# Late tiles of a mixture-of-experts kernel add the two parts of their up product on VectorE; one expert look-up; another front and end

## The reference

```python
ys = y * scale
d = rsqrt(einsum('bi,io->bo', ys * ys, weight * weight) + EPS)
xm = einsum('bsi,io->bso', x * ys[:, None, :], weight) * d[:, None, :]
...
router_logits = xm @ router_w.T + router_b + 0.1 * expert_weights    # from softmax(xm @ lang_w.T + lang_b)
top_p, top_i = top_k(softmax(router_logits), 2)                      # normalised to sum 1
h = gelu(einsum('bsd,edh->bseh', xm, w1) + b1)
expert_out = einsum('bseh,ehd->bsed', h, w2) + b2
return x + (top_p[..., None] * take_along_axis(expert_out, top_i[..., None], 2)).sum(2)
```

## Time and profile before

| | us |
|---|---|
| runs | 300.03, 297.01, 299.65 (median 299.65) |
| profiled execution | 296.99 |
| its span, first to last instruction | 295.2 |
| PE busy | 269.6 (91%) |
| PE weight loads busy | 221.2 (75%) |
| ACT, DVE, POOL busy | 195.2, 191.9, 175.4 |

### The profile page before, as it was taken

How to read it: one execution, slowest core, us unless ns; L and a number is a source line. 1 busy time by engine, 2 the same in 40 slices (tenths; PEclk the granted TensorE clock), 3 DMA queues, 4 the chain that set the end, 5 groups by cost and what they waited for, 6 DMA issues and landing times.

```text
span 295.2 us, 8972 instructions
## 1 busy us (share of the span) xinstructions
PE 269.6 (91%) x3065; PEld 221.2 (75%) x3065; DVE 191.9 (65%) x430; ACT 195.2 (66%) x425; POOL 175.4 (59%) x160
## 2 busy tenths in 40 slices
PE   7899967899999999999999999999999989999800
PEld 5778957788799998877778777777777767877500
DVE  2957787799999897656655655555656555556510
ACT  3355469499897997677667676766776756776500
POOL 8200026833366989887777877767787657464340
PEclk9799996999999999999999999999999999999985
DMA  6799995499862234645535555534535434332220
GB/s 160 290 400 388 368 323 155 129 404 450 294 191 41 38 59 69 95 76 88 93 56 91 75 93 73 79 68 76 90 59 80 88 56 74 53 39 25 32 35 1
DMA packets 39881, 39.53 MB, mean 134 GB/s; under 512 B 19920, under 2 KB 35744, under 8 KB 39680
## 3 DMA queue, kind: packets, MB, share of 16 engines
q1 hardware_dynamic: 32320, 28.56, 31.7%
q0 software_dynamic: 7488, 10.39, 21.9%
q10 hardware_dynamic: 32, 0.01, 0.0%
HBM read 27.61 MB, written 9.64 MB: 126 GB/s over the span
## 4 chain that ended last, share of the span: by engine, by line
PE 73%; DVE 9%; issue 6%; DMA 5%; POOL 4%; ACT 0%; DVEq 0%; POOLq 0%
PE ps L639 30%; PE ps L656 28%; DVE wsp L940 5%; PE ps L537 5%; DMA out<-onehot,idx 4%; PE ps L555 3%; POOL out L468 2%; PE ps L648 1%; POOL onehot L459 1%; PE ps L479 1%; PE ps L615 1%; DMA rows<-y_rows,idx 1%; PE ps L510 1%; PE ps L519 1%; DVE dv L871 1%
## 5 line engine op out<-in xcount | busy, mean ns | idle before, releaser
L639 PEld LDWEIGHTS ps<-onehot,wsp 128*128 (+1 forms) x1872 | 130.0, 98 | 37.4 <-issue 2.9
L639 PE MATMUL ps<-onehot,wsp 128*128 128x128 f16 x1872 | 154.4, 219 | 1.8 <-issue 1.5
L818 ACT ACTIVATE pay<-ps,cur 128x128 f32<-128x128 f32 x312 | 117.5, 463 | 54.9 <-issue 39.9
L656 PE MATMUL ps<-wsp,pay 128*128 (+1 forms) x616 | 139.4, 316 | 1.2 <-DVE pay L1102 1.2
L468 POOL DMA_INDIRECT out<-onehot,idx x39 | 68.7, 1762 | 28.9 <-POOL onehot L459 12.1
L1102 DVE SCALAR_TENSOR_TENSOR pay<-pay,cur 128x512 f16<-128x512 f32 x72 | 54.9, 762 | 28.8 <-ACT pay L806 26.6
L437 POOL DMA_INDIRECT rows<-y_rows,idx x39 | 49.4, 1266 | 22.4 <-issue 11.0
L459 POOL TENSOR_SCALAR onehot<-onehot,cur 128x256 f32<-128x256 f32 x37 | 43.0, 1161 | 25.6 <-DVE onehot L1120 21.6
L656 PEld LDWEIGHTS ps<-wsp,pay 128*128 128x128 f16 x616 | 45.3, 97 | 5.0 <-issue 1.6
L1096 DVE TENSOR_SCALAR pay<-pay,cur 128x512 f16<-128x512 f32 x36 | 19.4, 538 | 26.4 <-ACT pay L818 24.1
L806 ACT ACTIVATE pay<-pay,cur 128x512 f16<-128x512 f32 x36 | 26.0, 722 | 1.2
(11 more groups left out here) (177 smaller groups left out, 193.0 us busy)
## 6 DMA issues: line engine op xcount, KB each, us to landing
stage<-in_L_ffn_w SPq DMA_DIRECT2D x9, 1024.0 KB, 9.9
wsp<-in_L_ffn_w SPq DMA_DIRECT2D x7, 1024.0 KB, 11.8
y_rows<-pay SPq DMA_DIRECT2D x4, 512.0 KB, 9.4
wsp<-in_x SPq DMA_DIRECT2D x3, 512.0 KB, 8.1
b2bc<-in_L_ffn_b SPq DMA_DIRECT2D x1, 1024.0 KB, 9.4
rows<-y_rows,idx POOLq DMA_INDIRECT x39
out<-onehot,idx POOLq DMA_INDIRECT x39
wsp<-in_x SPq DMA_DIRECT2D x2, 256.0 KB, 5.8
```

The lines of the kernel that those rows point to most:

```text
L639: last = mm(ps[:, HB + (2 * j + g) % RING, c * P:(c + 1) * P], wsp[:, bass.ds(e, 1), o:o + P].rearrange("p a f -> p (a f)"), xsp[:, j % RI ...
L656: last = mm(ps[:, OB + j % 2, 0:width], hsp[:, (2 * j + g) % NH, part, c, :], wsp[:, bass.ds(e, 1), o + w:o + w + width].rearrange("p a f ...
L818: last = a.activation(to, ps[:, HB + (2 * j + g) % RING, c * P:(c + 1) * P], ACT.Gelu, bias=cur[:, j % CURS, cc:cc + 1], scale=cur[:, j % ...
```

## The change

- **Up, late tiles.** From tile LATE = 9 on, the second half (g = 1) takes x's high and low parts in one matmul of 256 columns, each part into PSUM columns of its own (banks 0 and 1): four matmuls instead of six. DVE adds the two (`sum_h`, a reduction of 128x1024 to 128x512 into `hsum`), and ACT's GELU reads `hsum` from SBUF. The first halves use banks 7 and 2, the rows banks 5, 6, 4 and 3 in turn (`LATE_H`, `LATE_O`). TensorE waits for `h_sum` before it writes the two banks again.
- **VectorE's order.** For late tiles `sum_h(j)`, `low_h(j, 0)`, then `rows_out(j - 2)` stand ahead of `high_h(j)`; before, `rows_out(j - 1)` and `low_h(j + 1, 0)` stood behind `low_h(j, 1)`.
- **Look-up.** BATCH is 31: all experts' numbers are read at once, on PE ahead of the loop.
- **Transposes.** TURNED is 7: tiles 7, 8 and 9 are turned by DMA.
- **Front.** Filler matmuls behind `sum_squares(0)` and `gram(2)`, ten instead of six behind `gram(3)`; the two DMAs of the probabilities go from the SP queue to POOL's; the weight half 7 is loaded ahead of them, `b2bc` ahead of the first gathers; the first up half stands ahead of the second transpose.
- **End.** For j = 36 and 37 the down half stands whole ahead of the up half; ACT weighs the last three tiles; the rows have five buffers (OUTS) instead of three.

```diff
+WIDE = range(E, NT)
...
+OUTS = 5
...
-WARM = 6
+WARM = 10
...
-TURNED = 10
+TURNED = 7
...
-EARLY = 8
-BATCH = 8
+BATCH = 31
+LATE = 9
+LATE_H = (7, 2)
+LATE_O = (5, 6, 4, 3)
...
+    hsum = stage[:, 0:2, 0:GH * P]
...
+    def bank_of_rows(j):
+        return OB + j % 2 if j < LATE else LATE_O[(j - LATE) % 4]
+
+    def bank_of_half(j, g):
+        return LATE_H[(j - LATE) % 2] if j >= LATE and g == 0 else HB + (2 * j + g) % RING
+
+
+    two_parts = ps[:, HB:HB + 2, :].rearrange("p b (c s n) -> p (b c) s n", s=2, n=P)
...
-        sp.wait_ge(p_ready, 1)
-        for b in range(NB):
-            sp.dma_start(y_tiles[:, b, :, D:ROW], payv[:, b * TB:(b + 1) * TB, D:ROW]).then_inc(p_written, 16)
         load_weights(7)
+        sp.wait_ge(p_written, 16 * NB)
+        sp.dma_start(b2bc[:, :, :].rearrange("p e d -> p (e d)"),
+                     b2.rearrange("(a e) d -> a (e d)", a=1).broadcast_to([P, E * D])).then_inc(b2_in, 16)
...
         load_weights(12)
-        sp.dma_start(b2bc[:, :, :].rearrange("p e d -> p (e d)"),
-                     b2.rearrange("(a e) d -> a (e d)", a=1).broadcast_to([P, E * D])).then_inc(b2_in, 16)
...
+        pool.wait_ge(p_ready, 1)
+        for b in range(NB):
+            g.dma_start(y_tiles[:, b, :, D:ROW], payv[:, b * TB:(b + 1) * TB, D:ROW]).then_inc(p_written, 16)
...
-            if j < NT - 2:
+            if j < NT - 3:
                 pool.wait_ge(o_read, j + 1)
-                g.tensor_scalar(outb[:, j % RING, :], outb[:, j % RING, :], cur[:, j % CURS, C_P:NCUR], None,
+                g.tensor_scalar(outb[:, j % OUTS, :], outb[:, j % OUTS, :], cur[:, j % CURS, C_P:NCUR], None,
                                 ALU.mult).then_inc(o_ready, 1)
                 pool.wait_ge(o_ready, j + 1)
             else:
-                pool.wait_ge(o_last, j - NT + 3)
+                pool.wait_ge(o_last, j - NT + 4)
...
         sum_squares(0)
+        pe.wait_ge(lg_read, T)
+        keep_warm(5, 1, 512)
...
         gram(2)
+        keep_warm(4, 1, 512)
         sum_squares(2)
...
         gram(3)
-        for _ in range(WARM):
-            mm(ps[:, RB, :], ones[:, :], onehot[:, 0:512], start=True, stop=True)
+        keep_warm(WARM, 1, 512)
...
+            if j >= LATE and g:
+                for w in range(2):
+                    for k in range(KD):
+                        o = w * HALF + k * F + (g * GH + c) * P
+                        last = mm(two_parts[:, c, 0:2 - w, :],
+                                  wsp[:, bass.ds(e, 1), o:o + P].rearrange("p a f -> p (a f)"),
+                                  xsp[:, j % RING, 0:2 - w, k, :], start=(w == 0 and k == 0), stop=(w == 1 and k == KD - 1))
+                return last
...
-            if j < EARLY:
+            if j not in WIDE:
                 steps = ((0, 0, D), (0, D, D), (1, 0, D))
...
                 elif g == 0:
                     wait_turned(pe, j)
+                elif j > LATE:
+                    pe.wait_ge(h_sum, j - LATE)
...
         transpose_rows(0)
+        blocks((0, 0), None)
         transpose_rows(1)
-        blocks((0, 0), None)
         blocks((0, 1), None)
         sum_squares(3)
         pe.wait_ge(te_ready, 1)
+        expert(E)
         for j in range(NT):
             if j + 2 < TURNED:
                 transpose_rows(j + 2)
-            blocks((j + 1, 0) if j + 1 < NT else None, (j - 1, 1) if j else None)
+            if NT - 4 < j < NT - 1:
+                blocks(None, (j - 1, 1))
+                blocks((j + 1, 0), None)
+            else:
+                blocks((j + 1, 0) if j + 1 < NT else None, (j - 1, 1) if j else None)
...
             if g == 0:
                 act.wait_ge(cur_ready, j + 1)
-            act.wait_ge(l1_done, 2 * j + g + 1)
+            if j >= LATE and g:
+                act.wait_ge(h_sum, j - LATE + 1)
...
+                up = (hsum[:, j % 2, :] if j >= LATE and g else ps[:, bank_of_half(j, g), :])[:, c * P:(c + 1) * P]
+                last = a.activation(to, up, ACT.Gelu,
                                     bias=cur[:, j % CURS, cc:cc + 1], scale=cur[:, j % CURS, C_GELU:C_GELU + 1])
...
+            if j == NT - 1:
+                weigh(NT - 3)
             gelus(j, 1)
...
+        def sum_h(j):
+            dve.wait_ge(l1_done, 2 * j + 2)
+            v.tensor_reduce(hsum[:, j % 2, :].rearrange("p (c n) -> p c n", c=GH), two_parts.rearrange("p c s n -> p c n s"),
+                            AX.X, ALU.add).then_inc(h_sum, 1)
...
-            if j >= RING:
-                dve.wait_ge(added, 16 * (j - RING + 1))
+            if j >= OUTS:
+                dve.wait_ge(added, 16 * (j - OUTS + 1))
...
         scale_weights(3)
         for j in range(NT):
-            if j == NT - 1:
+            if j >= LATE:
+                sum_h(j)
+                low_h(j, 0)
+            if LATE < j < NT - 2:
+                rows_out(j - 2)
+            if j >= NT - 3:
                 rows_out(j - 1)
             if j >= DIRECT:
                 high_h(j)
...
-            if 0 < j < NT - 1:
+            if 0 < j < LATE:
                 rows_out(j - 1)
-            if DIRECT <= j + 1 < NT:
+            if DIRECT <= j + 1 < LATE:
                 low_h(j + 1, 0)
```

More of the change, by code:

```diff
@@ L213, in adaln_moe @@
         xsp = onehot[:, 0:RING * 2 * D].rearrange("p (r s k n) -> p r s k n", r=RING, s=2, k=KD)
-        outb = onehot[:, RING * 2 * D:RING * 4 * D].bitcast(F32).rearrange("p (r n) -> p r n", r=RING)
+        outb = onehot[:, RING * 2 * D:(RING + OUTS) * 2 * D].bitcast(F32).rearrange("p (r n) -> p r n", r=OUTS)
         ps = ctx.enter_context(nc.psum_tensor("ps", [P, 8, 512], F32))
@@ L246, in adaln_moe @@
         gathered = [sem(f"gathered{r}") for r in range(ROWS)]
+        h_sum = sem("h_sum")
         t_done = sem("t_done"); turned = [sem(f"turned{r}") for r in range(RING)]; x_split = sem("x_split")
@@ L468, in _ @@
                 g.indirect_dma_start(out=out, out_offset=bass.IndirectOffsetOnAxis(ap=idx[:, j:j + 1], axis=0),
-                                     in_=outb[:, j % RING, :], in_offset=None,
+                                     in_=outb[:, j % OUTS, :], in_offset=None,
                                      compute_op=ALU.add).then_inc(added, 16)
@@ L638, in up_step @@
                     o = w * HALF + k * F + (g * GH + c) * P
-                    last = mm(ps[:, HB + (2 * j + g) % RING, c * P:(c + 1) * P],
+                    last = mm(ps[:, bank_of_half(j, g), c * P:(c + 1) * P],
                               wsp[:, bass.ds(e, 1), o:o + P].rearrange("p a f -> p (a f)"),
@@ L655, in down_step @@
                 for q, (part, w, width) in enumerate(steps):
-                    last = mm(ps[:, OB + j % 2, 0:width], hsp[:, (2 * j + g) % NH, part, c, :],
+                    last = mm(ps[:, bank_of_rows(j), 0:width], hsp[:, (2 * j + g) % NH, part, c, :],
                               wsp[:, bass.ds(e, 1), o + w:o + w + width].rearrange("p a f -> p (a f)"),
@@ L811, in gelus @@
                     act.wait_ge(cur_ready, j + 1)
-                act.wait_ge(l1_done, 2 * j + g + 1)
+                if j >= LATE and g:
+                    act.wait_ge(h_sum, j - LATE + 1)
+                else:
+                    act.wait_ge(l1_done, 2 * j + g + 1)
                 if j > DIRECT:
@@ L817, in gelus @@
                     to = hraw[:, (2 * j + g) % NH, c, :] if j < DIRECT else h32[:, g, c * P:(c + 1) * P]
-                    last = a.activation(to, ps[:, HB + (2 * j + g) % RING, c * P:(c + 1) * P], ACT.Gelu,
+                    up = (hsum[:, j % 2, :] if j >= LATE and g else ps[:, bank_of_half(j, g), :])[:, c * P:(c + 1) * P]
+                    last = a.activation(to, up, ACT.Gelu,
                                         bias=cur[:, j % CURS, cc:cc + 1], scale=cur[:, j % CURS, C_GELU:C_GELU + 1])
@@ L824, in weigh @@
             def weigh(j):
-                r = j % RING
+                r = j % OUTS
                 act.wait_ge(o_read, j + 1)
@@ L1105, in rows_out @@
             def rows_out(j):
-                r, e = j % RING, expert(j)
+                r, e = j % OUTS, expert(j)
                 if j == 0:
@@ L1114, in rows_out @@
                     return
-                v.scalar_tensor_tensor(out=outb[:, r, :], in0=ps[:, OB + j % 2, 0:D], scalar=cur[:, j % CURS, C_O:C_O + 1],
+                v.scalar_tensor_tensor(out=outb[:, r, :], in0=ps[:, bank_of_rows(j), 0:D], scalar=cur[:, j % CURS, C_O:C_O + 1],
                                        in1=b2bc[:, bass.ds(e, 1), :].rearrange("p a d -> p (a d)"),
-                                       op0=ALU.mult, op1=ALU.add).then_inc(o_read if j < EARLY else o_sum, 1)
-                if j >= EARLY:
-                    dve.wait_ge(o_sum, j - EARLY + 1)
-                    v.scalar_tensor_tensor(out=outb[:, r, :], in0=ps[:, OB + j % 2, D:2 * D], scalar=cur[:, j % CURS, C_O:C_O + 1],
+                                       op0=ALU.mult, op1=ALU.add).then_inc(o_sum if j in WIDE else o_read, 1)
```

(3 more changed lines are left out.)

## The result

The changed kernel takes 301.7 us (median of 300.01 to 303.06) against 298.33 us before in the same comparison: 1.0105 times, 95% interval 1.0066 to 1.0144. The forecast was 297.1 us, a gain of 0.84%. The direction was wrong; the time lies in the range only because that holds both signs.

What follows compares the result with a forecast made beforehand. Late tiles were taken as bound by issue, 2% above the array; look-ups -2.7, pace -0.9, transposes -0.7, front -1.0 and end +2.8 made -2.5 us: 294.5 from the profiled 297.0, or 297.1 off the median; range 293 to 303.

Steps and rivals of the forecast that it cites:

- The wide half: Late tiles' second up half, four matmuls instead of six: pace 5.34 us a tile, -0.9 us (from -2.5 to +3.1).
- The fifth rival: Late tiles: four matmuls save no issue, pace 5.49 with the wait, front's gain lost; +2.5, 302.2 us; chance 0.15.
- the lower bound: Late tiles: if every instruction counted alike, issue would take 4.91 us and the array's 5.28 would rule.
- Look-ups: Late tiles: three exposed look-ups go, -2.7 us; the load of 31 numbers is counted with the front.
- slack in the front: Near 58 us: 0.6 us of TensorE's wait for VectorE's splits and about 1 us of issue lead hide the load.
- Front: Up to the first tiles: first up product 1.5 us sooner, a loss of 0.5 for the load; -1.0 us in all.
- one fall of the clock: TensorE's granted clock, lower from 44.3 to 51.7 us; the lower level was to be gone from 44 to 52 us.
- that rival: POOL's queue: probabilities' copies at 5 us each make every gather 4.8 us late; +3.3, 303 us; chance 0.10.
- Transposes: Three tiles of four transposes leave a stretch where TensorE never idles: 3 x 0.22 = -0.7 us.
- End: Last scatters: VectorE reads tile 34's rows later, so a chain of five ends at 287.6 instead of 284.8: +2.8 us.
- the bound of 2.0: VectorE's strided sum in late tiles: 2.0 us at most, 1.21 taken; at 2.0, pace 5.52, +2.3, 302 us; chance 0.07.
- 81 ns for a pair of load and matmul: Thirty tiles: eight pairs fewer worth well over 10 us by this figure; rival that weight loads bind, 286 us, chance 0.03.

## Why the prediction went wrong

The view of what bounds the kernel held: late tiles are bound by issue, 2% above the array. But the 134 ns of a slot was an average that held the one separate wait too; without it 40 register instructions make 5.28 us. The failure is in what was made of it.

- **The wide half, the step that failed.** The prediction weighed "fewer instructions have to be fetched" against the new wait and took 5.34 us, below 5.39. The runs show 0.01 us for the first and 0.09 for the second, and the pace was 5.46. Over the stretch from tile 12 to 36 that is +1.9 us where -0.9 stood for all late tiles. The fifth rival, by which the wide half saves no issue, had this mechanism, this sign and, at 302.2 us, nearly the time, though part of its sum came from elsewhere. Its bound of 5.49 is 0.10 above today's 5.39, for the wait; against the lower bound, that all instructions count alike, the trace of before already spoke: most of its register instructions start 124 ns apart, whether one or two pairs of load and matmul follow. It should have carried the forecast.
- **Look-ups.** The 2.7 us came (2.6), and were paid back. For the load of 31 the prediction had both prices, 0.6 and 2.7 us, and took a loss of 0.5 on the ground of slack in the front. It cost 2.8 us, and 1.9 of them showed at tile 3. VectorE's load of 31 was left out of the sum altogether; tiles 9 to 12 took 1.0 us longer behind it, 0.44 in the half that waits and the rest because the issue-bound pace began three tiles sooner. With both loads cut back to eight this is gone; with TensorE's alone cut up, 0.4 us is left in one kernel and 0.9 in another.
- **Front.** TensorE's Gram sums ended 1.31 us after the first gather's issue instead of 2.36, but the first up half came only 0.24 us sooner, not 1.5. That is the transposes of tile 1, which now stand behind it: tile 1 then takes 3.32 us instead of 3.10, and without the load of 31 tile 3 stands where it stood (24.46 and 24.50 us after gather 0). Between the first half and tile 3 no wait of TensorE shows before, so its own work fills this stretch; the 0.58 us that the prediction read as a wait for VectorE's splits is idle time of the weight loads, ended by another step of VectorE (L923, `gram_max`). No run takes the earlier half 7, the fillers behind `sum_squares(0)` and `gram(2)` or the moved copies out one by one.
- **Clock and copies.** The prediction saw one fall of the clock; the earlier trace rows has another, in the second slice. Round the first gathers the clock was at the lower level for 6.8 us before and 3.4 after. Over all executions the old front had 6.8, 3.4, 6.8, 6.8 and 10.2 us there, the new one with six or ten fillers 3.4 five times and none three times, and with two fillers 6.8. So the new front goes with a shorter fall. In the three without one the first half comes 5.5 to 5.8 us after the gather instead of 6.2, but tile 9 no sooner for it (63.3 us without look-ups on TensorE, 64.2 and 65.6 with them). POOL's two copies took 2.08 us together and were hidden, so that rival comes to nothing here, and the stall that the Trainium skill warns of ("SBUF — State Buffer", SBUF: two separate sides) does not show.
- **Transposes.** -0.7 forecast; the half-tiles of tiles 6, 7 and 8 are 0.22, 0.11 and 0.22 shorter, about -0.55.
- **End.** +2.8 forecast (its own terms give the start of the chain as 4.2 and not 4.3 us after the pass, so +2.7), +2.3 measured, by the chain that the prediction describes; the rows sooner took 2.1 of it away.
- **`sum_h`** takes 1.23 us with its strided source, as a plain reduction of that size does; the bound of 2.0 was far off, and TensorE waits for it nowhere in the steady tiles.
- **The fixed rates.** The Trainium skill's 81 ns for a pair of load and matmul ("TensorE: Matmul & The Clock Gate", Back-to-back issue gap) would, by an estimate from it, have made the wide half worth over 10 us. With fixed addresses it is worth 0.02 us a tile, and pairs start 55 ns apart, so the trace disagrees.

In sum, -2.6 for the look-ups, +1.9 for the pace, +1.0 for tiles 9 to 12, +0.8 for the front with its transposes and TensorE's load, and +2.3 for the end make +3.4, where -2.7 - 0.9 - 0.7 - 1.0 + 2.8 = -2.5 stood. The wait, the load on VectorE and the order of the rows are each shown by a run that takes them out or cuts them; the front's share is not.

## What to carry to other kernels

Where addresses come from registers, count the sequencer's instructions: here each register instruction costs 0.13 us and each separate semaphore wait 0.1 us even if it is met, and matmuls between them are free until the array binds. A wait that another wait already implies, or that an engine with slack can take over, is then worth more than eight pairs of load and matmul (0.09 against 0.01 us a tile); moving one, with the look-ups out of the late tiles, made the kernel 1.2 to 1.5% faster than before. A load of numbers into registers costs by its count on every engine that makes it (0.7 us for 8, 2.8 to 3.0 for 31), so gathering loads into one only moved the price here.

## What the runs showed of the hardware that was not expected

- Register instructions on TensorE's queue come to 293, 294 and 298 in 40 us in three kernels with 40 or 48 of them a tile.
- A wait that is long met still costs 0.09 us of pace when it is an instruction of its own and issue binds; the next register instruction starts 230 ns after the last instead of 124. With fixed addresses two such waits a tile cost nothing. A wait that a register instruction carries itself shows no cost in the kernel before: it starts 124 ns after the one ahead, as others do.
- TENSOR_LOAD takes 2.8 us for 31 numbers on TensorE's queue and 3.0 on VectorE's, 0.09 us a number, and fixed addresses behind it give little lead: three of four loads of eight numbers placed there left gaps of 0.2 to 0.8 us.
